# Dense FFN stage: another order for the ramp and for the last tile of a chunk, and half of the second residual sums moved from PE and ACT to DVE

## What is computed

```python
def fp4_linear(x, w):                       # w_gate, w_up: 704 x 256, w_down: 256 x 704
    xq = fp4_quant_dequant(x)               # max of 16 -> scale -> nearest FP4 value * scale
    wq = fp4_quant_dequant(w)
    return jnp.einsum('bsk,nk->bsn', xq, wq)

def _L0_ffn_ref(x, w_gate, w_up, w_down):
    gate = fp4_linear(x, w_gate)
    y = fp4_linear(x, w_up)
    h = jax.nn.silu(gate) * y
    return fp4_linear(h, w_down)

x = _layernorm(x + _L0_attn_ref(x, ...))    # its last step: out @ Wo.T + bo
x = _layernorm(x + _L0_ffn_ref(x, w_gate, w_up, w_down))
x = _layernorm(x + _L1_attn_ref(x, ...))
x = _layernorm(x + _L1_ffn_ref(x, ...))
```

## Time and profile before

| | us |
|---|---|
| median of 3 runs | 3286.98 (3280.61 to 3294.07) |
| the profiled execution | 3285.37 |
| its span | 3283.6 |
| dense stage, from the attention's last instruction to the next stage's first | 388.0 |

### The profile page before, as it was taken

How to read it: one execution, slowest core, us unless ns; L and a number is a source line. 1 busy time by engine, 2 the same in 40 slices (tenths; PEclk the granted TensorE clock), 3 DMA queues, 4 the chain that set the end, 5 groups by cost and what they waited for, 6 DMA issues and landing times. The chain is left out here.

```text
span 3283.6 us, 66435 instructions
## 1 busy us (share of the span) xinstructions
PE 3015.9 (92%) x23140; PEld 1703.8 (52%) x23141; DVE 2384.8 (73%) x6464; ACT 1824.1 (56%) x2273; POOL 1437.5 (44%) x737
## 2 busy tenths in 40 slices
PE   4679999999999999999987899989999958999997
PEld 2233333333333333333333566556666748999996
DVE  5689999999999899999975788845665553333334
ACT  5236888888888888888886444432332223111112
POOL 3347787787778778787874001000011131111110
PEclk8788999999999999999999899989999979999999
DMA  5874443223444432344420111030000016555555
GB/s 139 197 203 115 94 83 85 74 67 79 96 96 86 84 72 74 71 96 96 99 67 9 34 26 31 1 103 1 15 17 21 20 55 199 181 179 185 181 178 203
DMA packets 201716, 304.68 MB, mean 93 GB/s; under 512 B 86208, under 2 KB 150560, under 8 KB 199264
## 3 DMA queue, kind: packets, MB, share of 16 engines
q1 hardware_dynamic: 192224, 277.73, 32.8%
q0 software_dynamic: 7632, 22.16, 1.9%
q10 hardware_dynamic: 1584, 1.21, 0.1%
HBM read 238.91 MB, written 62.13 MB: 92 GB/s over the span
## 5 line engine op out<-in xcount | busy, mean ns | idle before, releaser
L904 DVE CUSTOM_DVE_ANT_0 ps_r<-ps_r,toep 128x512 f32<-128x512 f32 x1894 | 1252.5, 715 | 74.6 <-PE ps_r L833 34.9
L1009 ACT ACTIVATE prob<-ps_s,csc 128x1024 f32<-128x1024 f32 x768 | 831.5, 1118 | 164.7 <-PE ps_s L857 142.6
L963 POOL TENSOR_TENSOR tb<-tb,toep 128x1024 f32<-128x1024 f32 x240 | 568.6, 2369 | 268.9 <-ACT tb L999 234.1
L833 PE MATMUL ps_r<-w 96*128 96x512 bf16 x1894 | 647.5, 383 | 8.1 <-DVE mp L904 4.1
L966 POOL TENSOR_TENSOR tb<-tb,mb 128x1024 f32<-128x1024 f32 x256 | 613.4, 2396 | 61.3 <-DVE tb L917 42.5
L873 PE MATMUL ps_o<-prob,vp 128*32 128x256 f32 x8192 | 549.9, 386 | 1.2 <-ACT prob L1006 0.9
L833 PEld LDWEIGHTS ps_r<-w 96*128 96x128 bf16 x1894 | 181.8, 97 | 403.7 <-DVE mp L904 256.2
L873 PEld LDWEIGHTS ps_o<-prob,vp 128*32 128x32 f32 x8192 | 214.1, 109 | 271.3 <-issue 178.1
L1807 POOL DMA_INDIRECT slots_scratch<-l_xh,l_place x64 | 63.2, 987 | 620.3 <-PE ps_lr L1833 389.1
L857 PE MATMUL ps_s<-p 120*128 120x512 bf16 (+1 forms) x1024 | 305.4, 382 | 30.7 <-DVE tb L917 15.1
L857 PE MATMUL ps_s<-w 120*128 120x512 bf16 (+1 forms) x1024 | 306.5, 381 | 10.7 <-ACT tb L999 9.2
(11 more groups left out here) (327 smaller groups left out, 3685.6 us busy)
## 6 DMA issues: line engine op xcount, KB each, us to landing
moe_w<-in_W_dram SPq DMA_DIRECT2D x71, 1024.0 KB, 5.3
w<-scr_scratch SPq DMA_DIRECT2D x176, 192.0 KB
mb<-mrow_scratch SPq DMA_DIRECT2D x16, 2048.0 KB, 8.0
scr_scratch<-part SPq DMA_DIRECT2D x64, 384.0 KB, 7.3
p<-scr_scratch SPq DMA_DIRECT2D x112, 192.0 KB
w<-scr_scratch SPq DMA_DIRECT2D x80, 128.0 KB
moe_pt<-slots_scratch SPq DMA_DIRECT2D x72, 132.0 KB, 2.1
vscr_scratch<-vsb SPq DMA_DIRECT2D x8, 1024.0 KB, 8.9
```

What stands on the lines that cost most here:

```text
L833: pe.matmul(ps_r[:, bank, :], buf[:, hh, 0, qt * P:(qt + 1) * P], buf[:, hh, 1, kc * CH:(kc + 1) * CH], start=True, stop=True)\
L904: dve.tensor_tensor_reduce(ps_r[:, bank, :], ps_r[:, bank, :], toep[:, col:col + CH], 1.0, -3.0e38, ALU.mult, ALU.max, mp[:, whose.par, hh ...
L963: pool.tensor_tensor(tb[:, k % DIAGS], tb[:, k % DIAGS], toep[:, col:col + CH].unsqueeze(1) .broadcast_to([P, 2, CH]), ALU.mult).then_inc( ...
L1009: act.activation(prob[:, n % RING], ps_s[:, mine % 2], ACT.Exp, scale=csc[:, qb * TB + kb:qb * TB + kb + 1]).then_inc(s["exp"], 1)
```

## The change

Three things change in `stage_dense`.

- **The ramp.** Of the second four first sums, tile 4 is taken before the weights of `down` are turned, and tiles 5 to 7 only behind `up(0)`. On ACT `size_rows(0)` moves in between the copies of the `down` weights; on DVE the add and statistics of tile 4 move in between steps 3 and 4 of `quantize_rows(0)`.
- **The last tile of a chunk.** On ACT `rows(c+1)` goes ahead of `size_hidden(i)`. On DVE the add of `out_rows(i+7)` goes from behind rounding step 3 to directly behind the product.
- **The second residual.** For tiles at places 2 and 3 the identity matmul and ACT's copy are left out; DVE adds `x1` to `ps_dd` itself, ahead of the statistics.

```diff
+        def by_dve(i):
+            return i % TPC >= 2
...
                 def down(i, turned):
...
-                    pe.matmul(ps_d[:, 0:D], ident[:], x1[:, i, :], start=True, stop=False)
+                    if not by_dve(i):
+                        pe.matmul(ps_d[:, 0:D], ident[:], x1[:, i, :], start=True, stop=False)
...
-                                       start=False, stop=(f == FT - 1))
+                                       start=(f == 0 and by_dve(i)), stop=(f == FT - 1))
...
                 for k in range(TPC):
-                    if k + 1 < TPC:
-                        turn_heads(k + 1, 0)
+                    turn_heads(k + 1, 0)
                     out_rows(k)
                     turn_up(k)
...
-                turn_heads(TPC, 0)
-                for k in range(TPC, 2 * TPC):
-                    if k + 1 < 2 * TPC:
-                        turn_heads(k + 1, 0)
-                    out_rows(k)
+                turn_heads(TPC + 1, 0)
+                out_rows(TPC)
...
-                turn_rows(0, 2 * TPC, 0)
+                turn_rows(0, TPC + 2, 0)
                 up(0)
+                for k in range(TPC + 1, 2 * TPC):
+                    if k > TPC + 1:
+                        turn_heads(k, 1)
+                    out_rows(k)
...
                 def summed(i):
+                    if by_dve(i):
+                        return
...
-                for k in range(TPC):
+                for k in range(TPC + 1):
                     heads(k)
                 root_z(0)
                 norm_z(0)
-                size_rows(0)
-                for k in range(TPC, 2 * TPC):
-                    heads(k)
+                heads(TPC + 1)
                 act.wait_ge(sw["ev"], up_to(len(gu)))
                 for f in range(FT):
                     act.wait_ge(sw["tr"], up_to(len(gu) + f + 1))
+                    if f == FT // 2:
+                        size_rows(0)
                     act.activation(wdn[0:rows_of(f), f, :], ps_t[0:rows_of(f), f % 2, 0:D], ACT.Copy).then_inc(sw["ev"], 1)
                 rows(0)
-                silu(0)
+                for k in range(TPC + 2, 2 * TPC):
+                    if k == TPC + 3:
+                        silu(0)
+                    heads(k)
...
-                    size_hidden(i)
+                    if t < TPC - 1:
+                        size_hidden(i)
...
                     if t == TPC - 1 and c + 1 < CHUNKS:
                         rows(c + 1)
+                    if t == TPC - 1:
+                        size_hidden(i)
...
                 def stats_d(i):
                     c, t = divmod(i, TPC)
+                    if by_dve(i):
+                        dve.wait_ge(s["down"], up_to(i + 1))
+                        if c >= 2:
+                            dve.wait_ge(s["dnorm"], up_to((c - 1) * TPC))
+                        dve.tensor_tensor(zd[:, c % 2, t, :], ps_d[:, 0:D], x1[:, i, :], ALU.add).then_inc(s["zd"], 1)
...
+                    if t == TPC - 1 and i - 1 + FAR < NT:
+                        add_rows(i - 1 + FAR)
                     dve.wait_ge(s["h"], up_to(i + 1))
...
+                                if t < TPC - 1:
+                                    add_rows(i - 1 + FAR)
                                 stats_z(i - 1 + FAR)
```

More of the change, by code:

```diff
@@ L1578, in keep_up, with add_rows @@
                     dve.tensor_copy(dst, up_bank(n % 5)[:, 0:many * P].rearrange("p (j n) -> p j n", n=P)).then_inc(sw["ev"], 1)
-                def stats_z(k):
+                def add_rows(k):
                     c, t = divmod(k, TPC)
@@ L1587, in stats_z @@
                     dve.tensor_tensor(z[:, c % 2, t, :], ps_y[:, 0:D], x[:, c % 2, t, :], ALU.add).then_inc(s["zc"], 1)
+                def stats_z(k):
+                    c, t = divmod(k, TPC)
                     dve.wait_ge(s["zc"], up_to(2 * k + 1))
@@ L1636, in _ @@
                 for k in range(TPC):
+                    add_rows(k)
                     stats_z(k)
@@ L1646, in _ @@
                     quantize_rows(0, k)
-                for k in range(TPC, 2 * TPC):
+                    if k == 3:
+                        add_rows(TPC)
+                        stats_z(TPC)
+                for k in range(TPC + 1, 2 * TPC):
+                    add_rows(k)
                     stats_z(k)
```

## The result

The changed kernel takes 3262.79 us (median of 6, 3256.99 to 3266.49) against 3282.93 us before (median of 6, 3279.97 to 3294.07). The ratio over the runs is 0.9931, 95% interval 0.9918 to 0.9944; the two medians alone give 0.9939. The forecast was 3262. The profiled execution has a span of 3264.7 us; the dense stage, from TensorE's first matmul in it to its first in the next stage, went from 383.04 us (1792.48 to 2175.52) to 363.97 (1787.03 to 2151.00). That is 19.1 us less, not the 23.4 of the sum.

What follows compares the result with a forecast made beforehand. PE was taken as the bound, busy 40.80 of a middle chunk's 41.94 us. Gains of 12.9, 4.3, 2.8, 2.0 and 1.4 sum to 23.4 us, taking 3285.4 to 3262 us; range 3254 to 3274.

Steps and rivals of the forecast that it cites:

- chunk ends: At seven chunk boundaries, `turn_rows` to `up` falls from 26.9 us in all to 14.0, gaining 12.9 us.
- clock at `up(28)`: At chunk 6's end, a shorter PE gap keeps full clock for `up(28)`, gaining 2.8 us.
- identity: In the five middle intervals, ten identity matmuls left out save PE 0.43 us each, 4.3 us.
- ramp: At the stage's start, the first product comes at 1832.0 instead of 1834.07, gaining 2.0 us.
- tail: At the stage's end, without the copy of tile 30 the norm and `down(31)` come earlier, gaining 1.4 us.
- a 2.35 us gap had been harmless: At chunk 0's end, matmuls ran at full clock after 2.35 us of idle PE, so the 2.8 counted as gained.
- DVE as the bound: Rival: in middle chunks DVE's slack of 1.2 us is eaten and DVE takes over; 3271 us, chance 0.15.
- Half clock for a whole chunk: Rival: behind the ramp the clock doesn't rise for one chunk; 3303 us, slower by 0.5%, chance 0.04.
- the stage about 365 us long: Sign for the whole dense stage, 388.0 us long in the profile before: about 365 us after the change.

Runs made afterwards that it cites:

- tile_only: The kernel before with only the new order of the last tile of a chunk; dense stage 367.90 us.
- ramp_tile: The changed kernel with the second residual back on TensorE and ScalarE in all tiles; dense stage 363.80 us.
- before_again: The kernel before once more, unaltered; dense stage 385.57 us.
- dve_only: The kernel before with only the second residual of two tiles in four moved to DVE; dense stage 388.28 us.
- ramp_tile_again: The changed kernel with the second residual as before, run a second time; 3265.74 us, ratio 0.9942, dense stage 368.79 us.
- warm_lean: The changed kernel with idle-filling matmuls in the tail and fewer of them in the ramp than warm_both; 3263.79 us, ratio 0.9934.
- after_again: The changed kernel once more, unaltered; 3267.55 us, ratio 0.9943, dense stage 364.13 us.
- keep_last: The changed kernel with the second residual of the last two tiles back on TensorE and ScalarE; 3266.49 us, ratio 0.9940.
- warm_both: The changed kernel with idle-filling matmuls in the ramp and in the tail; 3258.78 us, ratio 0.9925.

## Why the prediction was right, step by step

| term | forecast | measured | from |
|---|---|---|---|
| chunk ends | 12.9 | 14.0 | tile_only against before, up to `up(28)` |
| clock at `up(28)` | 2.8 | 2.8 | the same, `up(28)` to `up(31)` |
| identity | 4.3 | 2.8 | the change against ramp_tile, `up(4)` to `up(31)` |
| ramp | 2.0 | 2.0 | the change against tile_only, to `up(4)` |
| tail | 1.4 | -2.5 | the change against before |
| sum | 23.4 | 19.1 | |

- **Chunk ends**: right in mechanism and size; I put 2.0 us for the new distance and it is 1.9. Against before_again, where two `up`s of this stretch lost the clock, the same count gives 17.6. DVE's wait for `d_mf` is 0.26 us where I allowed 0.4, and its slack in front of the first product 1.4 where I had 1.2.
- **The clock at `up(28)`**: gained, but the reading was too narrow. It isn't that place's; the old chunk ends, with up to 3.6 us of idle PE, lose the clock now here, now there, by 0.5 to 2.8 us of the `up` behind them. The Trainium skill's page "TensorE: Matmul & The Clock Gate", section "What's actually happening", says that the chip's look at PE's activity runs freely and isn't started by the kernel; that gaps alike (1.90 us, or 2.42 and 2.43) end differently agrees with it. My argument that a 2.35 us gap had been harmless was one draw: in dve_only `out_rows` ran at half clock behind the same 2.35 us.
- **The identity**: the mechanism held, the size not. I counted ten at the full 0.43 us; for five of them a wait for `d_hT` took the place of the identity, and they gave 0.12. I had seen this cover for the last chunks alone.
- **The ramp**: `up(0)` came 26.2 us after the stage's start, forecast 26.0; at half clock to begin with, as put. `up(0)` took 6.67 us where I put 7.77, and the first product came 38.8 us after the start, forecast 39.5. I had not seen that `up(1)` would lose the clock as well. The 2.0 is one draw too: ramp_tile reached `up(4)` 2.4 us ahead of tile_only, ramp_tile_again 0.9 behind it.
- **The tail is the step that failed.** The moved norm did what was forecast: with the clock kept the tail is 24.52 us against 25.95, 1.43 less. The working left out that PE stands still for 2.43 us there and that the row of before was one outcome of two. It measured -2.5.
- **The rivals.** DVE as the bound came in a small measure: where GpSimd's add starts just ahead of a rounding step, that step takes three times as long. GpSimd and DVE in warm_lean:

```profile
1910.13 2.35 POOL L1260 TENSOR_TENSOR w<-w 128x1024 f32<-128x1024 f32 x1 [37.06 <-DMA w<-in_x_dram]
1910.27 2.97 DVE L1223 SCALAR_TENSOR_TENSOR d_vf<-d_h,d_fsc 128x704 f32<-128x704 f32 x1
```

0.89 has become 2.97. The Trainium skill's page "SBUF — State Buffer", section "Who interferes with whom", has DVE and GpSimd share a pair of ports that the first to start keeps for its whole instruction; the step's row agrees: it ends 0.76 us behind the add's end, and so, at 0.74 to 0.76, does every `d_vf` step that this add lengthened in the fourteen executions. With the residual on DVE this made one chunk 1.0 to 1.2 us longer in five of seven executions; ramp_tile, with 2.3 us of slack, took two such steps (3.02 and 2.82) at an unchanged 40.50. Half clock for a whole chunk did not occur.

That the time came within 0.8 us of the forecast although the sum was 4.3 too large is luck. The profiled execution of before, from which I subtracted, lay 2.4 us above the later median, the medians differ by 20.1 us where the stage gained 19.1, and the stages in front and behind, which the change does not touch, differ by more than that between executions (the stage began at 1782.9 to 1792.5 us, and 1108.1 to 1120.5 followed it). The sign "the stage about 365 us long" was not met either: it counts from the 388.0 of the earlier trace rows, and counted alike, with the 5 us ahead of the first matmul, the stage now takes 369. One stretch of the stage behind, 125 to 150 us after its start, in after_again and in ramp_tile, has clock 0.77 and 0.91:

```profile
2274.54:2299.54 25.00, 24.67 (x252) 17.12 (x248) 12.53 (x36) 5.32 (x10) 0.00 (x0) 0.77 0.01 2
```

```profile
2271.73:2296.73 25.00, 24.06 (x292) 17.23 (x292) 14.55 (x40) 6.41 (x12) 0.00 (x0) 0.91 0.01 1
```

What decides there, and at what moment a gap costs the clock, was not settled. No variant is shown to beat the change: ramp_tile_again, keep_last, warm_lean and warm_both have ratios of 0.9925 to 0.9942 with overlapping intervals. So the second residual on DVE is not shown to pay in the kernel's time; the new chunk ends carry the result.

## What to carry to other kernels

Before an operation is counted as saved, look at what its engine waits for next: if the engine then only arrives earlier at a wait, the saving ends there. Shifting work to another engine pays only once that engine no longer sets a wait; the same sixteen adds made PE idle 3.5 us longer at the old chunk ends, and moving them saved 2.8 us of the stage in the new order. And where PE idles for some 2 us ahead of dense work, one trace shows one draw of the clock: take both outcomes into the range, or fill the gap.

## What the runs showed of the hardware that was not expected

- The same program (the kernel before, and ramp_tile) went on at full clock behind the same idle gap on PE (1.90 us) in one execution and at half clock in the next.
- With three spare matmuls ahead of each of the last two products the clock stayed in all three executions (unfilled, in 3 of 11); they cost 0.5 us (tail 25.03 us, where the unfilled one takes 24.52 with the clock kept).
- A DVE rounding step of 0.89 us took 2.8 to 3.1 us when a GpSimd add had just started, and ended 0.75 us behind the add.
